# Last normalisation in place, output stored from the residual's tile, and five instruction lists in another order

## What is computed

```python
x_act = tanh(x)
static_out = einsum('bld,ed->ble', x_act, W)
# per head (16 heads of 16 columns), q = k = x_act, v = static_out:
#   S = lam * S;  u = beta * (v_t - S^T k_t);  S += k_t u^T;  o_t = S^T q_t
y = static_out + o
x = layernorm(x + (layernorm(y) * ln_gamma + ln_beta))
gate, up = x @ wg.T, x @ wu.T        # int weights / 127, hidden width 768
x = layernorm(x + (silu(gate) * up) @ wd.T)
```

## Time and profile before

| what | value |
|---|---|
| median of 3 runs | 1,717.36 us (1,714.75 to 1,728.76) |
| profiled execution | 1,734.76 us, its span 1,733.0 us |
| TensorE, VectorE, ScalarE, GpSimd busy | 1,373.0 (79%), 1,359.0 (78%), 1,118.9 (65%), 839.5 us (48%) |
| mean granted TensorE clock | 0.872 of full |
| DMA | 50.3% of 16 engines for the queue of SyncE, 187.56 MB |

### The profile page before, as it was taken

The page is one execution under the profiler, slowest core; times in us unless marked ns, Lnnn a source line. Parts: engine busy times, 40 slices in busy tenths (PEclk is TensorE's granted clock), DMA queues, the critical chain, the costliest instruction groups (busy, mean ns, idle before and its releaser), DMA issues.

```text
span 1733.0 us, 53678 instructions
## 1 busy us (share of the span) xinstructions
PE 1373.0 (79%) x21032; PEld 1070.7 (62%) x21032; DVE 1359.0 (78%) x3461; ACT 1118.9 (65%) x2357; POOL 839.5 (48%) x1106
## 2 busy tenths in 40 slices
PE   4358778888887888878888888888888878888765
PEld 3346666666666666666666666666666666666532
DVE  4578888888888788888888888888888888888731
ACT  3336667666766767666776666766766666776543
POOL 6024455445444545444455554444555444455542
PEclk9558989888988999888999998989998898898866
DMA  4555544555554555555555665654555655555200
GB/s 119 116 106 119 111 114 114 117 118 111 130 111 116 113 123 117 117 119 118 116 121 118 118 121 112 124 116 114 123 120 108 115 119 117 116 120 109 57 13 25
DMA packets 701325, 190.98 MB, mean 110 GB/s; under 512 B 620944, under 2 KB 688528, under 8 KB 701072
## 3 DMA queue, kind: packets, MB, share of 16 engines
q1 hardware_dynamic: 701072, 187.56, 50.3%
HBM read 103.55 MB, written 67.11 MB: 98 GB/s over the span
## 4 chain that ended last, share of the span: by engine, by line
DVE 24%; SPq 22%; DMA 16%; PE 15%; issue 11%; ACT 8%; POOL 3%; ACTq 0%; POOLq 0%; DVEq 0%
SPq L1060 9%; DMA scr_g<-gs 6%; DMA xa<-L_attn_x 6%; PE pg L253 4%; SPq L1073 4%; PE pc L182 4%; DVE tt L451 4%; PE pu L253 4%; SPq L995 3%; DVE gs L443 3%; DVE gate L495 2%; DVE xt L406 2%; DVE x1lo L488 2%; DMA y_out<-v 2%; DVE U L382 2%
## 5 line engine op out<-in xcount | busy, mean ns | idle before, releaser
L954 POOL TENSOR_TENSOR hlo<-gate,hhi 128x512 f16<-128x512 f32 x192 | 263.7, 1383 | 377.3 <-ACT hhi L784 375.4
L182 PE MATMUL pc<-R,tb 128*128 128x32 f16 x4096 | 158.2, 186 | 128.1 <-DVE R L372 125.2
L182 PEld LDWEIGHTS pc<-R,tb 128*128 128x128 f16 x4096 | 146.7, 118 | 148.9 <-DVE R L372 145.7
L182 PE MATMUL pc<-U,kb 128*128 128x32 f16 x4096 | 158.9, 188 | 95.4 <-DVE U L382 95.3
L182 PEld LDWEIGHTS pc<-U,kb 128*128 128x128 f16 x4096 | 146.9, 118 | 124.7 <-DVE U L382 124.6
L182 PEld LDWEIGHTS pc<-S,e 128*128 128x128 f16 x4096 | 151.9, 118 | 61.7 <-DVE S L399 55.9
L182 PE MATMUL pc<-S,e 128*128 128x32 f16 x4096 | 157.3, 186 | 38.8 <-DVE S L399 38.7
L279 PE MATMUL pd<-wd_t,hhi 128*128 128x256 f16 x768 | 178.2, 278 | 7.9 <-POOL hlo L954 5.6
L279 PE MATMUL pd<-wd_t,hlo 128*128 128x256 f16 x768 | 178.0, 278 | 0.0
L216 PEld LDWEIGHTS pf<-xb,e 128*128 128x128 f16 x4096 | 153.6, 118 | 32.9 <-DMA e<-scr_x 17.6
L216 PE MATMUL pf<-xb,e 128*128 128x32 f16 x4096 | 156.2, 191 | 18.5 <-DMA e<-scr_x 16.9
(11 more groups left out here) (134 smaller groups left out, 3229.0 us busy)
## 6 DMA issues: line engine op xcount, KB each, us to landing
xa<-L_attn_x SPq DMA_DIRECT2D x128, 128.0 KB
scr_x<-xt SPq DMA_DIRECT2D x64, 256.0 KB, 2.1
xb<-scr_x SPq DMA_DIRECT2D x256, 64.0 KB, 2.8
e<-scr_x SPq DMA_DIRECT2D x256, 64.0 KB, 3.5
scr_g<-gs SPq DMA_DIRECT2D x32, 512.0 KB, 3.5
gh<-scr_g SPq DMA_DIRECT2D x32, 512.0 KB, 3.4
kb<-k SPq DMA_DIRECT2D x512, 32.0 KB, 2.2
scr_t<-t SPq DMA_DIRECT2D x64, 256.0 KB, 3.5
```

Source lines behind the costliest of these rows:

```text
L182: last = pe.matmul(pc2[:, :, cols], stationary(h, a), moving[:, :, cols], start=a == 0, stop=a == 1)
L954: pool.tensor_tensor(hlo[:, t, :], gate[:, t % 2, :], hhi[:, t, :], ALU.subtract).then_inc(SEM["hl"], 1)
```

## The change

last_norm writes its result over x1 in xr (xa for the last chunk), and store_out sends that tile. The squares of x1's variance are dumped into v, not xr. The waits follow: first_norm, which writes xr, waits for the output of the chunk before; static_out waits for the variances that used its half of v, and for no output. The five lists get another order. Many lines of the diff move an item from the head of a list to its end under the next step number, which leaves the order alone; the diff below shows those whose neighbours change.

```diff
-        FIRST, LAST = -3, NS + 3
+        FIRST, LAST = -3, NS + 2
...
         def act_static_out(act, q, p, g):
             if g == 0:
                 act.wait_ge(SEM["res"], n_of("res", q - 2))
-                act.wait_ge(SEM["out"], n_of("out", q - 3))
+                act.wait_ge(SEM["va3"], n_of("va3", q - 3))
+            act.wait_ge(SEM["va2"], n_of("va2", q - 2, 2 * g + 2))
...
         def act_variance(act, q, p, z, n):
-            x_, to, nq, va = ((res, x1_of(q), nq2, va2), (x1_of(q), v[:, 1 - p], nq3, va3))[z - 2]
+            x_, to, nq, va = ((res, v[:, p], nq2, va2), (x1_of(q), v[:, 1 - p], nq3, va3))[z - 2]
...
-                elif z == 2:
-                    act.wait_ge(SEM["o"], n_of("o", q - 1))
-                elif q == NS - 1:
-                    act.wait_ge(SEM["out"], n_of("out", q - 2))
-                else:
+                elif z == 3 and q < NS - 1:
                     act.wait_ge(SEM["res"], n_of("res", q + 1))
...
         def act_first_norm(act, q, p, n):
             if n == 0:
                 act.wait_ge(SEM["nm2"], n_of("nm2", q))
+                if q < NS - 1:
+                    act.wait_ge(SEM["out"], n_of("out", q - 1))
...
         def act_last_norm(act, q, p, n):
-            act.activation(v[:, 1 - p, n, :], x1_of(q)[:, n, :], ACT.Identity, bias=nm3[:, n:n + 1],
+            act.activation(x1_of(q)[:, n, :], x1_of(q)[:, n, :], ACT.Identity, bias=nm3[:, n:n + 1],
...
         def sp_store_out(sp, q, p):
-                sp.dma_start(out[:, q * T + n * C:q * T + (n + 1) * C, :], v[:, 1 - p, n, :]).then_inc(SEM["out"], 16)
+                sp.dma_start(out[:, q * T + n * C:q * T + (n + 1) * C, :], x1_of(q)[:, n, :]).then_inc(SEM["out"], 16)
```

More of the change, by code:

```diff
@@ L306, in pe_step @@
             if live(s + 1):
+                pe_gram(pe, s + 1, 1 - p, 1, range(8, 16))
                 pe_gram(pe, s + 1, 1 - p, 2, range(0, 8))
@@ L311, in pe_step @@
                 pe_down(pe, s - 2, p, 0, range(0, 4))
-            if live(s + 1):
-                pe_gram(pe, s + 1, 1 - p, 3, range(0, 8))
             if live(s):
@@ L316, in pe_step @@
             if live(s + 1):
+                pe_gram(pe, s + 1, 1 - p, 3, range(0, 8))
                 pe_gram(pe, s + 1, 1 - p, 3, range(8, 16))
@@ L354, in pe_step @@
                 pe_keys_by_update(pe, s, p, 3)
+            if live(s - 1):
+                pe_up(pe, s - 1, 1 - p, 0)
+                pe_gate(pe, s - 1, 1 - p, 0)
+                pe_up(pe, s - 1, 1 - p, 1)
+                pe_gate(pe, s - 1, 1 - p, 1)
+                pe_gate(pe, s - 1, 1 - p, 2)
+                pe_up(pe, s - 1, 1 - p, 2)
+                pe_gate(pe, s - 1, 1 - p, 3)
+            if live(s + 1):
+                pe_keys_by_state(pe, s + 1, 1 - p, 0)
+            if live(s - 1):
+                pe_up(pe, s - 1, 1 - p, 3)
+                pe_gate(pe, s - 1, 1 - p, 4)
+            if live(s + 2):
+                pe_gram(pe, s + 2, p, 0, range(0, 8))
         def dve_rest_high(dve, q, p, w):
@@ L654, in dve_step @@
                 dve_state_high(dve, s, p, 3)
+                dve_state_sum(dve, s, p, 3)
+                dve_state_low(dve, s, p, 3)
+                dve_statistics(dve, s, p, 2)
+            if live(s - 1):
+                dve_multiply(dve, s - 1, 1 - p, 1)
+                dve_multiply(dve, s - 1, 1 - p, 2)
+            if live(s + 1):
+                dve_rest_high(dve, s + 1, 1 - p, 0)
+                dve_rest_sum(dve, s + 1, 1 - p, 0)
+            if live(s):
+                dve_statistics(dve, s, p, 3)
+                dve_moments(dve, s, p)
+            if live(s + 2):
+                dve_scale_keys(dve, s + 2, p, 0)
+            if live(s - 1):
+                dve_multiply(dve, s - 1, 1 - p, 3)
+            if live(s + 1):
+                dve_key_norms(dve, s + 1, 1 - p)
+            if live(s + 2):
+                dve_gram(dve, s + 2, p, 0)
+            if live(s - 1):
+                dve_multiply(dve, s - 1, 1 - p, 4)
+            if live(s + 1):
+                dve_rest_low(dve, s + 1, 1 - p, 0)
+            if live(s):
+                dve_load_residual(dve, s, p)
+            if live(s + 2):
+                dve_gram(dve, s + 2, p, 1)
+            if live(s - 1):
+                dve_multiply(dve, s - 1, 1 - p, 5)
+            if live(s + 1):
+                dve_store_inverse(dve, s + 1, 1 - p, 1)
         def act_rest(act, q, p, w):
@@ L976, in pool_step @@
[L976 to L987 removed]
+                pool_multiply(pool, s - 1, 1 - p, 3)
@@ new lines, in pool_step @@
+                pool_multiply(pool, s - 1, 1 - p, 4)
+                pool_multiply(pool, s - 1, 1 - p, 5)
+            if live(s):
+                pool_attention_norm(pool, s, p)
+            if live(s - 1):
+                pool_mean(pool, s - 1, 1 - p, 3)
+            if live(s):
+                pool_mean(pool, s, p, 2)
+            if live(s + 1):
+                pool_attention_out(pool, s + 1, 1 - p, 0)
+            if live(s - 1):
+                pool_bias(pool, s - 1, 1 - p, 3)
+            if live(s + 1):
+                pool_attention_out(pool, s + 1, 1 - p, 1)
@@ L990, in sp_load_x @@
+            if live(s):
+                pool_bias(pool, s, p, 2)
         def sp_load_x(sp, q, p):
```

209 lines of the change are left out of this document (75 added, 134 removed).

## The result

The changed kernel takes 1,755.7 us (median of 4 runs, 1,754.1 to 1,761.05) against 1,718.07 (4 runs, 1,714.75 to 1,728.76): ratio 1.0224, interval 1.0193 to 1.0254. It is slower; the forecast was 1,699, and the range ended at 1,725. The profiled execution has a span of 1,754.6 us.

What follows compares the result with a forecast made beforehand. No engine bounds alone: TensorE does from the gate matmul; ahead of it, late loads of x delay VectorE's nearly full list. Terms - 0.9 + 0.3 - 0.1 + 0.1 = - 0.6 us per step gave 1,699 us, range 1,673 to 1,725.

Steps and rivals of the forecast that it cites:

- keys_by_state 2 ahead of static_out 2: TensorE, window 2: two static_outs fill the wait for the residual; 0 at 2.4 GHz, + 0.9 us at 1.2 GHz.
- Mask to gate: From the Gram matrix's mask to the first gate matmul: - 0.9 us per step, gate at + 16.4 to + 16.7.
- Gram 0's wait for the spread keys: TensorE at Gram 0: keys come later and are wanted sooner, + 0.3 us per step, bounds 0 and + 1.3.
- Tanh waits for no load: ScalarE: tanh, moved behind update 2, finds x landed at + 5.7, ahead of its slot at + 6.3.
- load_x starts: SyncE's queue: the load of x waits for the square sums and can't start before 1.5 us ahead of the mask.
- the update starts: ScalarE, window 2: the update starts when its product is there, at mask + 4.3, not + 6.5 as in the late step.
- The output in place: static_out stops waiting for y_out, 0.15 us per step, already inside the idle time counted: 0 more.
- rival D: first_norm waits for the output, landing later: + 0.1 to + 0.6 us per step, 1,702 to 1,717 us; chance 0.08.
- Rival B: Gram 0 stalls for the spread keys where TensorE is the bound: slower, 1,729 to 1,741 us; chance 0.14.
- Rival A: Loads were late mostly in the profiled execution, so no change in the median: 1,709 to 1,717 us; chance 0.20.
- tanh's move: ScalarE: tanh goes behind update 2, static_out 0 and two variances, so the update needn't wait for it: gain 1.2 us per step.

Runs made afterwards that it cites:

- e1: The changed kernel with static_out 2 put back ahead of keys_by_state 2 on TensorE: 1,710.11 us, ratio 0.9944 to the kernel before.
- e8: e1 with all of TensorE's list in the order of before: 1,732.09 us, ratio 1.0049 to the kernel before.
- e3: The kernel before with only the in-place output tile and its waits, all lists as before: 1,711.47 us, ratio 0.9929.
- e4: The kernel before with tanh behind update 2 and static_out 0 ahead of the variances, tile as before: 1,790.39 us, ratio 1.0406.
- e5: e3 with tanh behind update 2, variance 1, static_out 0 and variances 2 and 3: 1,741.9 us, ratio 1.0111 to the kernel before.
- e12: e1 with load_residual behind Gram 1 on VectorE: 1,704.0 us, ratio 0.9888 to the kernel before.
- e7: e1 with VectorE's list from state_low 3 to multiply 5 in the order of before: 1,755.3 us, ratio 1.019 to the kernel before.
- e6: The changed kernel with static_out 2 issued a second time, ahead of keys_by_state 2: 1,709.21 us, ratio 0.9921 to the kernel before.
- e9: The changed kernel with static_out 2 and 3 both ahead of keys_by_state 2: 1,710.32 us, ratio 0.9932 to the kernel before.

## Why the prediction was wrong

**The step that failed** is "keys_by_state 2 ahead of static_out 2 ... both fit at 2.4 GHz: 0. At 1.2 GHz + 0.9, which no row there shows." At this place the kernel before has no row of the lower clock (granted 1.00 over the group in 27 of 27 steps), because the move itself makes the gap that brings it. The price could have been read elsewhere in that trace: the static_out at 338.51 takes 1.87 us, not 1.04. The item that I let pass ahead was waiting: keys_by_state waits for VectorE's state (L399), and static_out 2 was what TensorE did meanwhile. With 1.04 us of work moved out of that wait the idle time went from 0.67 to 1.56 us, a number that I could have had from the row of keys_by_state before (744.99, 0.67 idle) and the length of static_out. Measured: pair 3.4 us instead of 1.9, + 1.4 us for the inverse's product in 29 of 31 steps, and 29 x 1.4 = 41 us beside the 45.6 between the kernel after and e1. It is above my bound of 0.9 too. That term turns my sum of - 0.6 us per step into + 0.8, and the distance of the masks in the profiled executions did grow by 0.8.

**The rest of the sum** came out in size, in part by luck. In e1 the masks stand 49.3 us apart, 0.6 less than before, as my - 0.6. Mask to gate gave - 0.96 (forecast - 0.9) and gate to mask + 0.32 (32.87 against 32.55; forecast + 0.3). But Gram 0's wait for the spread keys, from which I had that + 0.3, isn't there. What is longer in e1 are TensorE's waits for VectorE's rest_low (131.8 us against 125.2) and for GpSimd's casts ahead of the down product (11.0 against 5.6).

**What held.** Tanh waits for no load (0.9 us at one place, 30.7 before). load_x starts at - 1.56 in the step shown (802.11 against the mask at 803.67), - 1.57 in the mean (forecast - 1.5). With the pair put back the update starts at + 4.23 (+ 4.3), the gate at + 16.67 (+ 16.4 to + 16.7). The output in place makes no wait for x1's norm: rival D has no row. The Trainium skill (DMA: Bandwidth & Descriptors, Anatomy of one DMA) left D no chance either. But its section is on transfers that GpSimd issues, and these are SyncE's, so my 2.3 us was worked out for another path than the one that took 5.0 us.

**Rival B** is slower too, but not this way: no wait of Gram 0 for the spread keys is left in the profile after. My + 0.3 for it was 0, and by e8 the new list of TensorE gains 0.7 us per step with the other new lists. So B's chance carried the right sign with a wrong mechanism.

**Rival A** is in part true. e1 has the forecast's gate and no loss from the pair, and is at 1,710, not 1,699. The gate matmul stood at + 17.63 in the mean of the profiled execution of before, so 0.96 us per step or 30 us should be gained; e1's span is 25.2 us under that execution's (1,707.8 against 1,733.0), but its median only 11.5 us under the median of before (1,710.11 against 1,721.6). The 13.7 us between the two are nearly all in how far that execution of before lay above its median (1,734.8 against 1,721.6, 13.2 us). That these were late loads, of which ordinary runs have fewer, would fit and was not shown. I had carried the ratio over as if both had the same.

**The output in place** was priced at 0, "inside the idle counted above". e3 measures 10 us (0.7%) for it with the lists as they were, so it gains where I let tanh's move take the credit; and tanh's move needs it (e4: 1.0406, e5: 1.0111).

**VectorE's cost** was taken as unchanged. It is busy 1,426.3 us for the same 3,461 instructions, 1,359.0 before, 67 us. My working moved items and kept their durations from rows where they stood beside other neighbours. rest_low (L372), which TensorE waits for, takes 608 ns in the mean against 458. Nothing shown here says that the growth costs more than a few us (e1, e12).

## What to carry to other kernels

Before letting an item pass another on an in-order engine, ask what the passed one was filling: if the item in front waits, the filler's length becomes idle time, and on TensorE what stands behind the idle time should be priced at the lower clock, even where the kernel before never shows that level at this place: here it came in 29 of 31 steps. Put wide products ahead of such a wait and narrow ones behind it. And when a change has many moves, look for the one whose undoing is one line: here 46 us hung on one place in TensorE's list, and the rest gained 11. When a reordered kernel is slower and no wait explains it, read the granted clock over the stretch where TensorE is the bound (e7, e8).

## What the runs showed of the hardware

**Idle time and clock.** With TensorE busy 2.30 of 4.20 us, 1.56 us of it idle ahead of keys_by_state 2, the clock was granted at 0.60 over the next 3.80 us; with a gap of 0.68 it was at 1.00 (e1, e6). Behind this gap the pair ran slow in 29 of 31 steps of the kernel after; at 1,213.14 the clock stayed at 1.00 behind the same work and the same gap. Eight extra products per step made the kernel 2.6% faster, 1,709.21 against 1,755.7. The Trainium skill (TensorE: Matmul & The Clock Gate, A second HAM failure mode: psum-queue depth-cycling) tells of a kernel whose clock goes to and fro because the engine idles shortly between groups of matmuls. By that, more idle time between the groups is a risk to the clock, and the trace agrees.

**Narrow products took as long at either level of the clock.** Groups of 32 products of 32 columns take 1.21 and 1.23 us in rows at the upper level and 1.25 at the lower (e9). Of 256 columns 8 take 1.04 us at the upper level and 1.87 at the lower (784.07 in e1, 338.51 in the kernel before). Of 512 columns 18 start in 3.80 us at the upper level and 9 at the lower (e1, e7).

**VectorE beside GpSimd.** Where the new order puts a VectorE operation with two inputs from SBUF beside GpSimd's, it lasts longer. The group of the residual's addition in the kernel after, then in e12 (busy us, mean ns, idle before):

```profile
L463 DVE TENSOR_TENSOR res<-res,lnb 128x1024 f32<-128x1024 f32 x32 | 66.2, 2068 | 0.9 <-DMA res<-L_attn_x 0.8
```

```profile
L465 DVE TENSOR_TENSOR res<-res,lnb 128x1024 f32<-128x1024 f32 x32 | 39.2, 1224 | 0.0
```

Such an addition in the kernel after, and what GpSimd does at that time:

```profile
989.38 2.18 DVE L463 TENSOR_TENSOR res<-res,lnb 128x1024 f32<-128x1024 f32 x1
```

```profile
988.00 2.49 POOL L954 TENSOR_TENSOR hlo<-gate,hhi 128x512 f16<-128x512 f32 x2
```

It took 1,373 ns in the mean before. With the residual's addition moved (e12) it takes 1,224, and VectorE is busy 27 us less in all than in e1 (1,394.0 against 1,421.4). The kernel's time moved by 6 us at most: in the stretch where it happens TensorE is the bound. The Trainium skill (GPSIMD Engine Reference, Specifications) has it that GpSimd shares its way to SBUF with VectorE, which is felt by VectorE's instructions with two inputs there. The trace agrees for L463 (2,068 and 1,224 ns, both inputs in SBUF).

The traces also tell in part when VectorE is slowed. In the kernel after the cast k (L412) takes 763 ns in the mean at 32 places where GpSimd isn't running, and 1,506 at the 29 where GpSimd's hlo (L954) is already running as it starts. In the kernel before GpSimd's L916 starts inside 28 of these casts, and they take 750. So in these rows VectorE's operation is the longer one where GpSimd was there first.
